# A two-layer graph network on one core: where tile 0's counts stand in the program, and how edge records are rounded

## The chip, the core and the metric

The kernel runs on one core of a Trainium2 chip. A core has five engines that each run their own instruction stream: TensorE (PE in the profile: matrix products and transposes), VectorE (DVE), ScalarE (ACT), GpSimd (POOL) and SyncE (SP, which here only issues transfers). They meet at semaphores. The metric is device microseconds (us) of one execution; lower is better.

## What is computed

There are 6250 nodes with 128 features and 200000 edges, sorted by destination. An attention layer comes first, then two rounds of a relational layer, each over the same edges:

```python
def layer0(h, src, dst, etype):
    e = leaky_relu(score_src[src] + score_dst[dst] + score_rel[etype], 0.01)
    m = segment_max(e, dst)                     # per destination node
    w = exp(e - m[dst])
    alpha = w / segment_sum(w, dst)[dst]
    agg = segment_sum(alpha[:, None] * h[src], dst)
    agg = where(deg > 0, agg, h)
    return agg + h @ loop_weight

x = layernorm(x + layer0(x, src, dst, etype))
h = x
for W_r, W_sl, W_el in two_rounds:
    self_msg = where(in_deg == 0, h @ W_el, h @ W_sl)
    msg = (rel_embed[etype] + h[src]) @ W_r
    h = rrelu(segment_sum(msg, dst) * deg ** -0.5 + self_msg)
return layernorm(x + h)
```

## The kernel before, in words

**Tiles and windows.** The nodes are cut into 50 tiles of 125 (`NT`, `TN`). The edges that end in tile t lie in a window of 4224 edges (`WIN`), held as 128 partitions of 33 columns (`C`). The main loop runs over the tiles; the order of work on every engine is written out by hand, and nothing reorders it.

**What a tile t of the main loop does.** GpSimd gathers the source rows of the window, one indirect transfer for each of the 33 columns (L568), into one of two row buffers; the gathers of tile t wait for the last products of tile t-2 (`acc_c`), since both use the same buffer. SyncE loads the lists of the window: small copies in `load_lists`, and copies of destination and type lists spread to all partitions in `load_wide` (L459). TensorE makes the edge terms with one-hot matrices (`terms`, L781 to L783), ScalarE copies them out, SyncE stores them to memory (L464) and loads them back in another shape (L469, `drw`). On VectorE `terms(t)` (L1146) waits for that load. `weights(t)` (L1156 to L1175) computes the segment maximum, with two short steps on TensorE in between (L870, L875), up to `z`. ScalarE takes the exponent and scales 33 one-hot tiles (L684), TensorE accumulates the attention sum with them (L884, 33 products recorded as 66). VectorE then builds the one-hot lists of the next tile: `prepare_wide(t+1)` (L1109 to L1116, then three L1101) before the sum is read, `prepare_edges(t+1)` (L1131 to L1142) after. `finalize(t)` and `normalise(t)` (L1195 to L1197) give the first layer's output of the tile.

**Counts.** The relational rounds need, for each tile, a matrix that counts edges from every node to the 125 of the tile. It is built in seven batches, `batch(t, 0)` to `batch(t, 6)`: VectorE makes two one-hot tensors for each (L1124 with `idx`), TensorE multiplies them (L814), ScalarE copies the result into the one buffer `AT` (L590, L625, L626), and `store_counts(t)` on SyncE writes `AT` to memory (L475, L477). The first batch of tile t on ScalarE waits for the store of tile t-1 (`at_stored`) and for TensorE's `row(t-1)` (L845 to L847), which also reads `AT`. Products leave TensorE through two pairs of PSUM banks in turn; each use waits for the copy two uses earlier (`before(n)`), in the order of the table `SEQ`.

**Edge records.** The counts are built from records of all edges, made once. `records` on VectorE turns source and destination numbers into two small numbers each (L1251 to L1261, ten instructions on 125 x 1600 elements, from the start of L1251 to `terms(0)`); SyncE stores them (L512); before tile 2's gathers GpSimd fetches them in ten indirect transfers (L560, `recw`); VectorE brings them into shape (L1294, two instructions for each of ten blocks), TensorE transposes them (L899) and ScalarE writes `idx` (L590).

**Where tile 0 stands.** Tile 1's gathers come before the ten transfers of records, tile 2's after. In the loop's first turn, after tile 0's sum and `prepare_edges(1)`, VectorE, TensorE and ScalarE turn the records into `idx` and build tile 0's seven batches, and only then begin `normalise(0)` and tile 1's `terms(1)` and `weights(1)`. SyncE stores tile 0's counts in the same turn, ahead of the lists of tile 3.

**After the loop** TensorE multiplies the stored counts with the node features, twice over (L960), reading them back in pieces; this part runs from about 2160 us to the end.

Of the kernel before, what the change touches and what calls it, by code (L numbers as in the profile page):

```python
# [7 lines left out]
I32 = mybir.dt.int32  # L8
# [5 lines left out]
P = 128  # L14
# [43 lines left out]
SHIFT = 128.0  # L58
NBK = 2
# [45 lines left out]
for t_ in range(NT):  # L105
    if t_ + 1 < NT:
        for k_ in range(QK):
            SEQ["dr", t_ + 1, k_] = len(SEQ)
    if t_ == 0:
        SEQ["types", 1] = len(SEQ)  # L110
        SEQ["turned", 1] = len(SEQ)
        for b_ in range(NGB):
            SEQ["idx", b_] = len(SEQ)
    for j_ in range(BT):
        SEQ["cnt", t_, j_] = len(SEQ)
        if 1 <= t_ < NT - 1 and j_ == 2:
            SEQ["types", t_ + 1] = len(SEQ)
        if 1 <= t_ < NT - 1 and j_ == 3:
            SEQ["turned", t_ + 1] = len(SEQ)
    if t_ in EARLY:  # L120
        SEQ["early", t_] = len(SEQ)
# [29 lines left out]
def build(nc, x, src, dst, etype, emb_rel, loop_w, fc_w, fc2_w, rel_emb, W_r, W_sl, W_el, out):  # L151
    ctx = ExitStack()
    with ctx:
# [96 lines left out]
        lo = carve([P, EW])  # L250
        q_i = lo.bitcast(I32)
        qf = carve([P, EW])
        off = carve([P, EW])
# [123 lines left out]
        def seq(*key):  # L377
            return SEQ[key]
# [5 lines left out]
        def slot(n):  # L384
            return bank[2 + 2 * (n % NBK)]

# [52 lines left out]
        def sp_fast(sp):  # L439
# [73 lines left out]
            for t in range(NT):  # L513
                if t + 2 < NT:
                    f2 = window(t + 2)
                    load_lists(t + 2, f2)
                    load_wide(t + 2, f2)
                if t in EARLY:
                    load_early(t)
                if t + 1 < NT:  # L520
                    reshape_terms(t + 1)
                else:
                    for m in range(RD):
                        load_piece(m)
                if t < NT - 1:
                    store_x1(t)
                store_counts(t)
# [60 lines left out]
        def act_evac(act, n, o, i):  # L588
            act.wait_ge(s("pb"), n + 1)
            act.activation(o, i, ACT.Copy).then_inc(s("ev"), 1)  # L590

        def act_fast(act):
# [79 lines left out]
            for t in range(NT):  # L672
# [19 lines left out]
                if t == 0:  # L692
# [3 lines left out]
                    for b in range(NGB):  # L696
                        n = seq("idx", b)
                        act_evac(act, n, idx[:, b * GB:(b + 1) * GB, :], slot(n)[:, :].rearrange("p (m g) -> p g m", g=GB))
                    for j in range(BT):
                        batch(0, j)  # L700
                    node_t(0)
                    node_a(0, 0)
                elif t < NT - 1:
                    for j in range(3):
                        batch(t, j)
# [48 lines left out]
        def pe_fast(pe):  # L754
# [106 lines left out]
            for t in range(NT):  # L861
# [27 lines left out]
                if 1 <= t < NT - 1:  # L889
                    row(t - 1)  # L890
                if t == 0:
                    types_in(1)
                    types(1)
# [7 lines left out]
                    for j in range(BT):  # L901
                        batch(0, j)
                    x1_in(0)
# [162 lines left out]
        def dve_fast(v, link):  # L1066
# [180 lines left out]
            def records():  # L1247
                v.wait_ge(s("st_l16"), 64)
                v.wait_ge(s("ld_src"), 32)
                a, b, c, i_ = qf[0:EP], lo[0:EP], off[0:EP], srcl[0:EP]  # L1250
                link(v.tensor_scalar(a, i_, 1.0 / TN, -0.496, ALU.mult, ALU.add))  # L1251
                link(v.tensor_copy(q_i[0:EP], a))
                link(v.tensor_copy(a, q_i[0:EP]))
                link(v.scalar_tensor_tensor(b, a, -float(TN), i_, ALU.mult, ALU.add))
                link(v.tensor_scalar(c, b, 0.0, None, ALU.is_lt))
                link(v.tensor_tensor(a, a, c, ALU.subtract))
                link(v.tensor_scalar(c, b, float(TN), None, ALU.is_ge))
                link(v.tensor_tensor(a, a, c, ALU.add))
# [10 lines left out]
            for t in range(NT):  # L1269
# [14 lines left out]
                if t == 0:  # L1284
                    finalize(0)
                    prepare_edges(1)
                    for b in range(NGB):
# [11 lines left out]
                    normalise(0)  # L1299
                elif more:  # L1300
# [11 lines left out]
                else:  # L1312
# [611 lines left out]
```

## Time and profile before

| what | us |
|---|---|
| median of 3 runs | 2772.72 |
| lowest and highest of them | 2772.16, 2774.16 |
| the profiled execution's own time | 2772.09 |
| span of its profile | 2770.1 |
| share of the span: PE, DVE, POOL, ACT | 78%, 74%, 57%, 44% |

The profile follows one execution. Its span begins with the first instruction and ends with the last, so 1.99 us of the execution lie around it. A timeline row gives start, duration, engine, source line, operation and tiles, then how often the row repeats and, in brackets, how long the engine had been idle before it and what released it. A row that stands for several instructions gives the time from the start of the first to the end of the last. DMA_INDIRECT on POOL is the time that GpSimd takes to issue a gather, not the time that the data takes. A row of SPq is the issue of a transfer by SyncE.

### The profile page before, as it was taken

To read this page: it belongs to the slowest core of one execution; us is meant where nothing else is said; L and a number is where in the kernel's file an instruction comes from. 1 tells how busy PE (TensorE), PEld (TensorE's weight loads), DVE (VectorE), ACT (ScalarE), POOL (GpSimd) and SP (SyncE) were. 2 spreads that over 40 slices of the span, in tenths; PEclk is the share of its full clock that TensorE was granted. 3 is DMA by queue.
4 is the path that set the end of the run, shared out by engine and by line. 5 is a ranking of instruction groups with operands and counts; after the bars stand their busy time and mean duration, and the time that the engine had idled before them with its cause. 6 is when DMAs were issued, how large, how long until landed. Compare 5 with 4: busy or idle time off the path is not lost.

```text
span 2770.1 us, 45483 instructions
## 1 busy us (share of the span) xinstructions
PE 2148.2 (78%) x16208; PEld 1803.9 (65%) x16208; DVE 2044.5 (74%) x4582; ACT 1222.7 (44%) x3215; POOL 1590.8 (57%) x1672
## 2 busy tenths in 40 slices
PE   1467666677677677787787788788787999999998
PEld 0355555566566566576676677667666876888887
DVE  6889998888888888898888888888887456333333
ACT  1265566555455555555555555555654323000000
POOL 6767777777777777777777777777774000000000
PEclk9888888888888888888889988999898999999999
DMA  8535554454554554554555555555444344666664
GB/s 222 164 117 166 174 172 141 149 176 146 157 181 145 157 182 150 154 184 152 166 176 157 169 175 164 172 169 174 154 153 153 108 157 135 215 209 212 215 211 158
DMA packets 184632, 463.50 MB, mean 167 GB/s; under 512 B 86336, under 2 KB 113784, under 8 KB 164577
## 3 DMA queue, kind: packets, MB, share of 16 engines
q1 hardware_dynamic: 116050, 339.10, 36.3%
q0 software_dynamic: 53600, 114.17, 15.8%
q10 hardware_dynamic: 14752, 7.26, 1.0%
q8 instruction: 132, 2.16, 0.3%
q14 instruction: 98, 0.80, 0.1%
HBM read 362.54 MB, written 97.84 MB: 166 GB/s over the span
## 4 chain that ended last, share of the span: by engine, by line
POOL 52%; PE 24%; issue 18%; DVE 4%; DMA 2%; ACT 0%; POOLq 0%; ACTq 0%; SPq 0%; DVEq 0%
POOL arena L568 52%; PE pair L960 19%; PE bank L884 1%; DVE arena L1124 1%; PE bank L845 1%; PE pair L933 1%; DMA wlp<-n_L_gnn_loop_weight_dram 1%; PE pair L963 1%; DMA group_starts<-endv 0%; DMA arena<-in_x_dram,srcw 0%; DVE arena L1101 0%; PE pair L814 0%; PE pair L791 0%; DVE arena L1071 0%; DVE arena L1072 0%
## 5 line engine op out<-in xcount | busy, mean ns | idle before, releaser
L568 POOL DMA_INDIRECT arena<-rows,srcw x1617 | 1540.4, 953 | 510.1 <-issue 492.2
L1124 DVE TENSOR_TENSOR arena<-bank,idx 128x2000 bf16<-128x2000 bf16 (+3 forms) x700 | 560.5, 853 | 22.4 <-PE pair L814 19.0
L960 PE MATMUL pair<-arena 125*125 125x384 bf16 x3285 | 551.4, 326 | 1.6 <-DVE arena L1325 1.6
L814 PE MATMUL pair<-arena 128*128 128x250 bf16 x2500 | 344.5, 285 | 262.2 <-DVE arena L1124 208.7
L590 ACT ACTIVATE arena<-pair 99x264 f32<-99x264 f32 (+2 forms) x410 | 278.8, 712 | 582.6 <-PE pair L814 448.9
L960 PEld LDWEIGHTS pair<-arena 125*125 125x125 bf16 x3285 | 447.4, 136 | 103.3 <-issue 8.4
L684 ACT ACTIVATE arena<-arena,wexp 128x128 f32<-128x128 bf16 x1650 | 487.4, 387 | 1.6
L884 PE MATMUL bank<-arena 128*125 128x130 f32 x3300 | 486.9, 319 | 0.0
L884 PEld LDWEIGHTS bank<-arena 128*125 128x125 f32 x3300 | 476.4, 230 | 3.9
L814 PEld LDWEIGHTS pair<-arena 128*128 128x128 bf16 x2500 | 237.8, 102 | 339.7 <-DVE arena L1124 271.5
L1101 DVE TENSOR_TENSOR arena<-arena,bank 128x4224 bf16<-128x4224 int16 x150 | 344.2, 2350 | 1.7
L1323 DVE SCALAR_TENSOR_TENSOR arena<-pair,norm,arena 125x128 f32<-125x128 f32 x99 | 34.6, 350 | 315.3 <-PE pair L963 270.9
L845 PE MATMUL bank<-arena 125*125 125x384 bf16 x1275 | 219.4, 330 | 2.1 <-DVE arena L1213 2.1
L845 PEld LDWEIGHTS bank<-arena 125*125 125x125 bf16 x1275 | 171.0, 137 | 45.2 <-issue 13.9
L791 PE MATMUL pair<-arena 128*125 128x200 bf16 x1650 | 191.8, 288 | 10.1 <-DVE arena L1124 10.1
L791 PEld LDWEIGHTS pair<-arena 128*125 128x125 bf16 x1650 | 190.1, 167 | 12.7 <-issue 10.8
L731 ACT ACTIVATE rstd<-mv,epst 125x1 f32<-125x1 f32 x50 | 14.7, 294 | 406.6 <-DVEq L1365 406.6
L1124 DVE TENSOR_TENSOR arena<-bank,et 128x6600 bf16<-128x6600 bf16 x50 | 179.2, 3584 | 0.0
L625 ACT ACTIVATE arena<-pair 128x500 bf16<-128x500 f32 x150 | 95.7, 638 | 71.9 <-PE pair L814 71.4
L1156 DVE TENSOR_TENSOR u<-arena,dr 128x33 f32<-128x33 f32 x50 | 10.7, 214 | 151.0 <-DMA arena<-rows,srcw 150.8
L1124 DVE TENSOR_TENSOR arena<-bank,dl 128x4224 bf16<-128x4224 bf16 x50 | 117.9, 2358 | 1.7
L804 PE MATMUL bank<-onesb,arena 128*125 128x1 bf16 x50 | 11.4, 229 | 131.1 <-issue 128.6
(250 smaller groups left out, 2311.5 us busy)
## 6 DMA issues: line engine op xcount, KB each, us to landing
arena<-counts SPq DMA_DIRECT2D x106, 812.5 KB, 4.4
counts<-arena SPq DMA_DIRECT2D x50, 1562.5 KB
arena<-dst SPq DMA_DIRECT2D x50, 1056.0 KB
arena<-etype SPq DMA_DIRECT2D x50, 1056.0 KB
arena<-rows,srcw POOLq DMA_INDIRECT x1617
arena<-counts SPq DMA_DIRECT2D x14, 281.2 KB, 2.7
edge_terms<-arena SPq DMA_DIRECT2D x200, 12.4 KB
xt<-in_x_dram SPq DMA_DIRECT2D x50, 62.5 KB
```

The lines of the kernel that those rows point to most:

```text
L568: pool.indirect_dma_start(out=rows[:, q, c, :], out_offset=None, in_=rows0, in_offset=bass.IndirectOffsetOnAxis(ap=srcw[:, q, c:c + 1], ax ...
L590: act.activation(o, i, ACT.Copy).then_inc(s("ev"), 1)
L625: act.activation(AT[:, :, d0:d0 + 2 * G], two, ACT.Copy)
L684: r = act.activation(hot[:, c, :], hotb[:, c, :], ACT.Copy, scale=wexp[:, c:c + 1])
L791: r = pe.matmul(b_[0:TN, 0:R], hotb[:, c, 0:TN], toh[:, c, :], start=(c == 0), stop=(c == C - 1))
L814: r = pe.matmul(group_of(n, gi), ohl[:, sl, gi * GC + c, :], ohm[:, sl, gi * GC + c, :], start=(c == 0), stop=(c == GC - 1))
L845: pe.matmul(o, AT[0:TN, h, :], hs0[0:TN, h, :], start=(h == 0), stop=False)
L884: r = pe.matmul(sums[0:TN, 0:D + 2], hot[:, c, 0:TN], rows[:, q, c, 0:D + 2], start=(c == 0), stop=(c == C - 1))
L960: r = pe.matmul(o, ring[0:TN, m % RD, h - h0, :], hs[k][0:TN, h, :], start=(h == first), stop=(h == last - 1))
L1101: return v.tensor_tensor(out_.rearrange("p (j t) -> p j t", t=2), list_.rearrange("p (j t) -> p j t", t=2), two[:, None, :].broadcast_to(s ...
L1124: return v.tensor_tensor(hot_.rearrange("p c (j t) -> p c j t", t=2), iotap[:, 0:w].rearrange("p (j t) -> p j t", t=2)[:, None, :, :].broa ...
L1323: link(v.scalar_tensor_tensor(o, b_[0:TN, 0:D], n_, acc[0:TN, t, :], ALU.mult, ALU.add))
```

## The change

Two things are changed. First, the step from records to `idx` and the seven batches of tile 0 move from the loop's first turn into its second, on VectorE, TensorE and ScalarE. They now stand behind tile 1's attention weights and sum and behind tile 2's edge terms, and ahead of `row(0)` and of tile 1's own batches. The store of tile 0's counts moves on SyncE behind the lists and edge terms of the second turn; the table `SEQ` follows. Second, `records` rounds the quotient by adding and subtracting 12582912 in one instruction; the six instructions that converted it to integer and back and corrected it by one are gone.

```diff
@@ SEQ
     if t_ == 0:
         SEQ["types", 1] = len(SEQ)
         SEQ["turned", 1] = len(SEQ)
+        continue
+    if t_ == 1:
         for b_ in range(NGB):
             SEQ["idx", b_] = len(SEQ)
+        for j_ in range(BT):
+            SEQ["cnt", 0, j_] = len(SEQ)
@@ SyncE, turn t
                 if t + 1 < NT:
                     reshape_terms(t + 1)
+                    if t == 1:
+                        store_counts(0)
...
-                store_counts(t)
+                if t >= 1:
+                    store_counts(t)
@@ ScalarE, turn t
-                    for b in range(NGB):
-                        n = seq("idx", b)
-                        act_evac(act, n, idx[:, b * GB:(b + 1) * GB, :], slot(n)[:, :].rearrange("p (m g) -> p g m", g=GB))
-                    for j in range(BT):
-                        batch(0, j)
                     node_t(0)
                     node_a(0, 0)
                 elif t < NT - 1:
+                    if t == 1:
+                        for b in range(NGB):
+                            n = seq("idx", b)
+                            act_evac(act, n, idx[:, b * GB:(b + 1) * GB, :], slot(n)[:, :].rearrange("p (m g) -> p g m", g=GB))
+                        for j in range(BT):
+                            batch(0, j)
@@ TensorE, turn t
                 if t + 1 < NT:
                     terms(t + 1)
-                if 1 <= t < NT - 1:
-                    row(t - 1)
-                if t == 0:
-                    types_in(1)
-                    types(1)
+                if t == 1:
                     for b in range(NGB):
                         n = seq("idx", b)
...
                     for j in range(BT):
                         batch(0, j)
+                if 1 <= t < NT - 1:
+                    row(t - 1)
+                if t == 0:
+                    types_in(1)
+                    types(1)
                     x1_in(0)
                     x1_node(0)
@@ VectorE, records
                 link(v.tensor_scalar(a, i_, 1.0 / TN, -0.496, ALU.mult, ALU.add))
-                link(v.tensor_copy(q_i[0:EP], a))
-                link(v.tensor_copy(a, q_i[0:EP]))
-                link(v.scalar_tensor_tensor(b, a, -float(TN), i_, ALU.mult, ALU.add))
-                link(v.tensor_scalar(c, b, 0.0, None, ALU.is_lt))
-                link(v.tensor_tensor(a, a, c, ALU.subtract))
-                link(v.tensor_scalar(c, b, float(TN), None, ALU.is_ge))
-                link(v.tensor_tensor(a, a, c, ALU.add))
+                link(v.tensor_scalar(a, a, TO_WHOLE, TO_WHOLE, ALU.add, ALU.subtract))
@@ VectorE, turn t
                 if t == 0:
                     finalize(0)
                     prepare_edges(1)
+                    normalise(0)
+                if t == 1:
                     for b in range(NGB):
...
                     for j in range(BT):
                         batch(0, j)
-                    normalise(0)
-                elif more:
+                if t >= 1 and more:
                     for j in range(2):
                         batch(t, j)
```

VectorE before, at the end of the loop's first turn: the last one-hot tensors of tile 0's batches, then `normalise(0)` and the edge terms and weights of tile 1 (`u` is their first step).

```order
L1124 TENSOR_TENSOR arena<-bank,idx 128x1500
L1124 TENSOR_TENSOR arena<-bank,idx 128x768
L1195 RECIPROCAL norm<-nv 125x1
L1196 RECIPROCAL nv<-nv 125x1
L1197 TENSOR_SCALAR arena<-arena,mv,nv 125x128
L1146 TENSOR_TENSOR dr<-drw 128x33
L1147 TENSOR_TENSOR dr<-dr,drw 128x33
L1156 TENSOR_TENSOR u<-arena,dr 128x33
```

VectorE in the changed kernel, at the same place: the last steps of `prepare_edges(1)` lead straight into `normalise(0)` and tile 1's terms.

```order
L1147 TENSOR_TENSOR Kx<-dstB 128x32
L1148 TENSOR_SCALAR FS<-dstB 128x33
L1149 TENSOR_SCALAR LS<-dstB 128x33
L1202 RECIPROCAL norm<-nv 125x1
L1203 RECIPROCAL nv<-nv 125x1
L1204 TENSOR_SCALAR arena<-arena,mv,nv 125x128
L1153 TENSOR_TENSOR dr<-drw 128x33
L1154 TENSOR_TENSOR dr<-dr,drw 128x33
L1163 TENSOR_TENSOR u<-arena,dr 128x33
```

The record steps (L1297 now) and the fourteen one-hot tensors of tile 0 that stood between these two places come behind `prepare_wide(2)`.

TensorE before, from the end of tile 1's edge types to tile 1's weights: 40 transposes of records and 50 products of tile 0's counts stand between them.

```order
L798 MATMUL pair<-identb,ctd 128x125
L799 MATMUL pair<-identb,ctd 72x125
L899 MATMUL pair<-ident,arena 128x128 x40
L814 MATMUL pair<-arena 128x250 x50
L833 MATMUL bank<-ident,arena 128x125
L837 MATMUL bank<-wall,nT 125x384
L762 MATMUL bank<-ident,xt 128x125
L870 MATMUL bank<-ident,lf 1x128
```

TensorE in the changed kernel, after tile 2's edge terms (the last of them is the first row) and up to tile 1's own counts and tile 2's edge types.

```order
L789 MATMUL pair<-arena,Zr 3x264
L901 MATMUL pair<-ident,arena 128x128 x40
L820 MATMUL pair<-arena 128x250 x50
L851 MATMUL bank<-arena 125x384
L852 MATMUL bank<-relW,arena 125x384
L853 MATMUL bank<-relW,arena 125x384
L820 MATMUL pair<-arena 128x250 x24
L797 MATMUL pair<-arena 125x200 x33
```

The 90 instructions have moved past tile 1's sum and tile 2's terms, and `row(0)` (L851 to L853) now waits behind them.

SyncE before, from the edge terms of tile 1 into the second turn.

```order
L464 DMA edge_terms<-arena 3x1056 x4
L469 DMA drw<-edge_terms 128x3x33
L481 DMA dense_input<-arena 125x128
L475 DMA counts<-arena 128x6250
L477 DMA counts<-arena 128x250
L444 TENSOR_LOAD plan_i
```

SyncE in the changed kernel, from the edge terms of tile 2 to the end of the second turn.

```order
L466 DMA edge_terms<-arena 3x1056 x4
L471 DMA drw<-edge_terms 128x3x33
L477 DMA counts<-arena 128x6250
L479 DMA counts<-arena 128x250
L483 DMA dense_input<-arena 125x128
L477 DMA counts<-arena 128x6250
L479 DMA counts<-arena 128x250
```

Tile 0's counts have moved one turn on: two stores of counts now stand in the second turn, with only the small store of `dense_input` between them.

## Rows read from the trace of the kernel before

**Rows 1.** The page: shares by engine of the chain that ended last

```profile
POOL 52%; PE 24%; issue 18%; DVE 4%; DMA 2%; ACT 0%; POOLq 0%; ACTq 0%; SPq 0%; DVEq 0%
```

**Rows 2.** Waits of POOL: who waited for whom, total us, times, longest

```profile
POOL arena L568 <- PE bank L884: 9.1, 1, 9.1
```

**Rows 3.** Timeline of POOL: first fetch of records, first gathers of tiles 3 and 4

```profile
115.44 0.98 POOL L560 DMA_INDIRECT arena<-edge_records,gidx  x1 [3.19 <-DMA edge_records<-arena]
...
178.12 0.94 POOL L568 DMA_INDIRECT arena<-rows,srcw  x1 [9.07 <-PE bank L884]
...
219.46 0.94 POOL L568 DMA_INDIRECT arena<-rows,srcw  x1 [0.30 <-issue]
```

**Rows 4.** Timeline of DVE in `records` and at the start of `terms(0)`

```profile
94.44 0.99 DVE L1252 CAST arena<-arena 125x1600 int32<-125x1600 f32 x1
...
98.36 0.99 DVE L1255 TENSOR_SCALAR arena<-arena 125x1600 f32<-125x1600 f32 x1
...
104.14 1.83 DVE L1259 SCALAR_TENSOR_TENSOR arena<-arena 125x1600 f32<-125x1600 f32 x1
...
107.61 0.19 DVE L1146 TENSOR_TENSOR dr<-drw 128x33 f32<-128x33 f32 x1
```

**Rows 5.** Timeline of SyncE's queue: terms of tiles 0, 1, 2 and the records

```profile
99.97 0.39 SPq L469 DMA_DIRECT2D drw<-edge_terms  x1
107.73 0.76 SPq L512 DMA_DIRECT2D edge_records<-arena  x2
...
128.37 2.02 SPq L464 DMA_DIRECT2D edge_terms<-arena  x4
139.73 0.39 SPq L469 DMA_DIRECT2D drw<-edge_terms  x1
...
180.36 1.32 SPq L464 DMA_DIRECT2D edge_terms<-arena  x4
190.07 0.39 SPq L469 DMA_DIRECT2D drw<-edge_terms  x1
```

**Rows 6.** Chain that ended last, two transfers waited for: start, us

```profile
38.00 2.79 DMA gst<-group_starts
...
2075.82 2.58 DMA arena<-rows,srcw
```

**Rows 7.** Timeline of DVE from the end of `prepare_edges(1)` to `terms(2)`

```profile
134.21 0.35 DVE L1294 TENSOR_SCALAR arena<-arena,kcol 128x256 f32<-128x256 f32 x1
...
147.32 0.42 DVE L1237 COPY idx<-arena 128x100 bf16<-128x100 bf16 x2 [1.41 <-ACT arena L590]
...
158.86 0.15 DVE L1195 RECIPROCAL norm<-nv 125x1 f32<-125x1 f32 x1
...
159.37 0.19 DVE L1146 TENSOR_TENSOR dr<-drw 128x33 f32<-128x33 f32 x1
...
162.59 0.35 DVE L1204 SCALAR_TENSOR_TENSOR arena<-bank,iso,slt 125x128 f32<-125x128 f32 x1 [1.94 <-ACT slt L650]
...
166.07 0.29 DVE L1109 TENSOR_TENSOR arena<-xt,bank 125x128 f32<-125x128 f32 x1
...
175.25 0.41 DVE L1237 COPY idx<-arena 128x100 bf16<-128x100 bf16 x2
...
198.15 0.18 DVE L1146 TENSOR_TENSOR dr<-drw 128x33 f32<-128x33 f32 x1
```

**Rows 8.** Timeline of PE: record transposes, sums of tiles 1 and 2

```profile
139.48 2.04 PE L899 MATMUL pair<-ident,arena 128*128 128x128 f32 x12
...
167.75 9.61 PE L884 MATMUL bank<-arena 128*125 128x130 f32 x66
...
179.23 0.38 PE L845 MATMUL bank<-arena 125*125 125x384 bf16 x1
...
187.79 1.85 PE L814 MATMUL pair<-arena 128*128 128x250 bf16 x8 [6.12 <-DVE arena L1124]
...
205.88 9.44 PE L884 MATMUL bank<-arena 128*125 128x130 f32 x66
```

More of the change, by code:

```diff
@@ L58 @@
 SHIFT = 128.0
+TO_WHOLE = 12582912.0
 NBK = 2
@@ L249, in build @@
         here(AT_AT)
-        lo = carve([P, EW])
-        q_i = lo.bitcast(I32)
         qf = carve([P, EW])
-        off = carve([P, EW])
         here(1536)
@@ L1249, in records @@
                 v.wait_ge(s("ld_src"), 32)
-                a, b, c, i_ = qf[0:EP], lo[0:EP], off[0:EP], srcl[0:EP]
+                a, i_ = qf[0:EP], srcl[0:EP]
                 link(v.tensor_scalar(a, i_, 1.0 / TN, -0.496, ALU.mult, ALU.add))
-                link(v.tensor_copy(q_i[0:EP], a))
-                link(v.tensor_copy(a, q_i[0:EP]))
-                link(v.scalar_tensor_tensor(b, a, -float(TN), i_, ALU.mult, ALU.add))
-                link(v.tensor_scalar(c, b, 0.0, None, ALU.is_lt))
-                link(v.tensor_tensor(a, a, c, ALU.subtract))
-                link(v.tensor_scalar(c, b, float(TN), None, ALU.is_ge))
-                link(v.tensor_tensor(a, a, c, ALU.add))
+                link(v.tensor_scalar(a, a, TO_WHOLE, TO_WHOLE, ALU.add, ALU.subtract))
                 v.scalar_tensor_tensor(recs[0:EP, :, GRAN:2 * GRAN], a.rearrange("p (j r) -> p j r", r=GRAN), -float(TN),
@@ L1311, in dve_fast @@
                         batch(t, j)
-                else:
+                if not more:
                     finalize(t)
```

## The prediction

> **What bounds the kernel now.** Read the chain that ended last first. GpSimd holds 52% of it, TensorE 24% [rows 1]: the gathers of the main loop set the pace, and the products after the loop set the rest. So an edit on VectorE or TensorE in the loop counts only where GpSimd waits for it. The waits of GpSimd come next: in the whole loop it waits once for another engine, 9.1 us for TensorE's L884 [rows 2]. The timeline of GpSimd places that wait: the gathers of tile 3 start at 178.12 us, after 9.07 us idle [rows 3]. They need the buffer of tile 1, and tile 1's sum on TensorE ends at 167.75 + 9.61 = 177.36 [rows 8]. From the end of a sum to the first gather it releases is therefore 178.12 - 177.36 = 0.76 us. From there on GpSimd never waits, so its clock at the first gather of tile 4, 219.46 us [rows 3], sets all that follows. The gathers of tile 3 take 219.46 - 178.12 = 41.34 us.
>
> The second thing to read is how near the next such wait is. Tile 4 needs tile 2's sum, which ends at 205.88 + 9.44 = 215.32 [rows 8]. GpSimd could have begun at 216.08, and began at 219.46: **3.38 us** of slack. If the change brings tile 1's sum forward but leaves tile 2's where it is, the wait of 9.07 us only moves to tile 4, and what is gained is those 3.38 us and no more. So the sum below has to find the end of tile 2's sum.
>
> **The records, four instructions in place of ten.** From the start of the second instruction (94.44) to the start of the ninth (104.14) are 9.70 us [rows 4]. One instruction comes back there, a TENSOR_SCALAR on the same shape with 0.99 us [rows 4], about 1.02 with its hand-over. VectorE is 8.7 us shorter and stands at `terms(0)` at 107.61 - 8.7 = 98.9. Should the new one run as slowly as the two-input form (1.83 us [rows 4]) it is 99.8. Neither matters, because `terms(0)` waits for `drw`, whose load is issued only at 99.97 [rows 5], after SyncE's wait for the edge terms; nothing in the change touches that. What it takes to land is not in the trace, as VectorE always came later. The nearest rows are two transfers that were waited for, 2.58 and 2.79 us [rows 6]. I take 2.6 (bounds 2 to 4, four for a queue that is still draining lists). `terms(0)` then starts at 102.6: **5.0 us** early, and not 8.7. All of tile 0's weights and sum shift by 5.0.
>
> SyncE's store of the records was issued at 107.73, when they were ready [rows 5]. It now follows the load of `drw` directly, at about 100.4. In the trace it took 115.44 - 107.73 = 7.7 us until GpSimd went on [rows 3, 5], so it has landed at 108 and the wait of 3.19 us [rows 3] goes. GpSimd then begins the ten fetches at 115.44 - 3.19 = 112.3 or sooner. At its pace of 41.34 / 33 = 1.25 us for one transfer it ends them at 124.8, tile 2's gathers at 166.1 and, if tile 1's sum is done, tile 3's at 207.5. That is 8 us before the release worked out below, so GpSimd's own work has no price.
>
> **Tile 1's weights ahead of tile 0's counts.** The legs, one after the other:
> - `terms(1)` needs its own `drw`. SyncE issued it at 139.73, after 11.36 us from the store of the terms at 128.37 [rows 5]. These follow TensorE, which is 5.0 early: 134.7, and 137.3 with the landing. VectorE, which before began the records at 134.21 [rows 7], is through with `prepare_edges(1)` at 129.2 and, after 0.5 for `normalise(0)` (158.86 to 159.37 [rows 7]), at `terms(1)` at 129.7, so it idles 7.6 us. The transfer is the bound here, which the counts had hidden.
> - From `terms(1)` to the end of `weights(1)`: 166.07 - 159.37 = 6.70 us, of it 1.94 waiting for `slt` [rows 7]. That step of tile 0's node is now made while the transfer is under way, so I take 6.70 - 1.94 + 0.1 = 4.9: 142.2. Upper bound 6.7, if TensorE's small steps are slower after its idle time.
> - To the end of tile 2's edge terms on TensorE: 179.23 - 166.07 = 13.16 [rows 7, 8]: 155.3. Tile 1's sum ends at 177.36 - 23.9 = 153.5, so GpSimd, ready near 166, no longer waits for it.
> - `prepare_wide(2)` ends 9.2 us after the weights, at 151.4, and VectorE can shape only two blocks of records ahead. It waits for TensorE until 155.3. From the first transposes to the copy for tile 0's first batch: 147.32 - 139.48 = 7.84 [rows 7, 8], and I add 0.2 for the copies of the edge terms out of the same PSUM banks: 163.3.
> - Tile 0's batches: 158.86 - 147.32 = 11.54 [rows 7]: 174.9.
> - From tile 1's first batch to `terms(2)`: 198.15 - 175.25 = 22.90 [rows 7]: **197.8**, where the kernel before has 198.15.
>
> So almost all that VectorE is given back it waits away again: 3.7 us at the first `drw`, 7.6 at the second, some 4 for TensorE ahead of the transposes. Tile 2's sum ends 0.35 earlier, at 214.97, and the gathers of tile 4 start at 215.73: 219.46 - 215.73 = **3.7 us** gained. Tile 2's sum ended 215.32 - 177.36 = 38.0 us after tile 1's, the gathers of a tile take 41.3, so there is no third wait, and the gain reaches the end of the loop and the products after it. Against the profiled execution, 2772.09 - 3.7 = 2768.4; its own time lies 0.63 under the median, so against the median 2772.72 - 3.7 = **2769.0**.
>
> **What is costed at nothing.** The store of tile 0's counts has ScalarE's `AT` as its price. It is issued when the last copy is made, near 177, and the store of the same size took 7.7 us [rows 3, 5], so it lands near 184.7. ScalarE's first copy for tile 1 waits for it. TensorE's third batch of tile 1 needs that copy (about 1 us), and before started at 187.79 because VectorE's one-hot tensor was late [rows 8]; now it would be 187.4. The store may land as late as 186.4: 1.7 us of cover. On SyncE nothing but the small store of `dense_input` and tile 1's counts are queued behind it. `row(0)` stands behind the counts and shares this cover.
>
> **The skill and the landing.** The Trainium skill, "DMA: Bandwidth & Descriptors", section "Anatomy of one DMA — SWDGE (gpsimd) path", puts the fixed cost of a transfer issued by GpSimd at about 2.0 us. The trace has 2.58 and 2.79 for small ones [rows 6], a little more. By the page's figure, both landings would be 0.6 shorter, and as an estimate the gain would be 4.9 and not 3.7.
>
> **Rivals.**
> - *The second `drw` comes sooner.* Tile 1's terms took 11.36 us from store to load; tile 2's took 190.07 - 180.36 = 9.71 [rows 5]. Tile 1's list copies overlapped the last of the ten record fetches, which in the changed kernel are issued 3.2 us earlier or more while the lists come 5 us earlier, so much of the overlap stays. At 9.71 the gain is 3.7 + 1.65 = 5.4, with landings of 2.2 us 6.2: about 2766.5. For it: one row at 9.71. The most it could be is where GpSimd itself bounds tile 4, 219.46 - 207.5, some 12 us, and VectorE's own work forbids that.
> - *The hand-overs eat it.* Weights at 6.7 in place of 4.9, a landing of 3 us or more, transposes that wait for more copies: 1.8 + 0.8 + 0.8 = 3.4 us, and the gain is about 0.3. The time is then 2772.4. For it: TensorE is idle before tile 1's weights.
> - *The count store becomes the wait (slower).* `AT` is one buffer and its two uses now lie 0.4 us apart on VectorE. Each us that the store lands after 186.4 delays TensorE's third batch, then the types behind it, and VectorE, by one. The gain is gone at 190.1, 13 us after the issue; a loss of 5.5 us needs 195.6, 18.6 after it. The list copies of a tile took up to 11.4 with all else in flight [rows 5], so I hold it unlikely: 2778 at that point.
> - *The new rounding does nothing for the path.* That is part of my forecast for 3.7 of its 8.7 us; with the old ten instructions the whole chain would be 5.0 later, tile 4 would start at 220.8, and the kernel would be 1.3 slower than before. So the two edits need each other.
>
> **How the numbers follow.** A measurement tells about 0.2%, 5.5 us, from no change. Forecast, a gain of 1 to 5.5: 0.60. Sooner `drw`, a gain over 5.5: 0.20. Hand-overs, from a gain of 1 to a loss of 5.5: 0.16. Slower by over 5.5, the store: 0.04. So faster 0.20, same 0.76, slower 0.04. The range reaches from a gain of 8 (2764.7) to a loss of about 0.5 (2773.2), which leaves out half of the extreme cases on either side.
>
> **What the profile after would show.** VectorE idle some 3.7 us before its first L1153 (`terms(0)`), and some 7 before the second. Tile 1's sum over near 153.5. GpSimd without a wait at tile 3 and with one wait for TensorE at tile 4, of about 8 us (more if the gathers beside the records are issued faster); tile 4's first gather near 215.7. ScalarE's first copy of tile 1's counts behind the store, TensorE's third batch near 187.4. Wrong would be: no wait at tile 4 (gain above 11), a start of tile 4 after 219.5 (a loss), or a further wait of GpSimd in a later tile, which would mean that the loop is not as loose behind tile 4 as I read it.

## The result and the profile after

| what | before | after |
|---|---|---|
| median, us | 2773.84 | 2769.09 |
| lowest and highest, us | 2769.97, 2775.00 | 2766.67, 2770.64 |
| runs | 22 | 22 |
| the profiled execution | 2772.09 | 2769.03 |
| span of its profile | 2770.1 | 2767.0 |

The ratio after to before is 0.9985, with a 95% interval of 0.9979 to 0.9991. The changed kernel is some 4.7 us faster (2.5 to 5.8), which is less than the 0.2% that was named as the bound for "no change". The two profiled executions differ by 3.1 us. One execution of all those reported here, of `records_terms_first_b` below, ran slow (3030.98 us, at a granted TensorE clock of 0.726 of full speed where the others have 0.905 to 0.908), and its median is taken without it.

The chain that ended last kept its shares to within a point; this row answers to [rows 1]:

```profile
POOL 52%; PE 25%; issue 18%; DVE 3%; DMA 1%; ACT 0%; SPq 0%; POOLq 0%; DVEq 0%; ACTq 0%
```

The waits of GpSimd (who waited for whom, total us, times, longest) answer to [rows 2], and its timeline to [rows 3]:

```profile
POOL arena L573 <- PE bank L890: 12.8, 1, 12.8
...
POOL arena L565 <- DMA edge_records<-arena: 1.1, 1, 1.1
```

```profile
108.14 0.94 POOL L565 DMA_INDIRECT arena<-edge_records,gidx  x1 [1.07 <-DMA edge_records<-arena]
...
120.64 0.94 POOL L573 DMA_INDIRECT arena<-rows,srcw  x1 [0.30 <-issue]
...
215.61 0.95 POOL L573 DMA_INDIRECT arena<-rows,srcw  x1 [12.76 <-PE bank L890]
```

There is still exactly one wait for TensorE, but it stands at tile 4 (215.61) and no longer at tile 3. It is longer than before, 12.76 us and not 9.07, and GpSimd is nevertheless earlier: 219.46 - 215.61 = 3.85 us at tile 4's first gather. A longer wait is no loss when it replaces a later start.

The timeline of VectorE, from `records` to tile 2's terms, answers to [rows 4] and [rows 7]. L1153 is the first step of `terms`, L1116 the first step behind the weights, L1297 the shaping of the records, L1244 the first step of a batch:

```profile
94.17 0.99 DVE L1259 TENSOR_SCALAR arena<-arena 125x1600 f32<-125x1600 f32 x1
...
96.94 1.82 DVE L1262 SCALAR_TENSOR_TENSOR arena<-arena 125x1600 f32<-125x1600 int32 x1
101.80 0.19 DVE L1153 TENSOR_TENSOR dr<-drw 128x33 f32<-128x33 f32 x1 [3.03 <-DMA drw<-edge_terms]
...
135.48 0.19 DVE L1153 TENSOR_TENSOR dr<-drw 128x33 f32<-128x33 f32 x1 [6.94 <-DMA drw<-edge_terms]
...
140.85 0.28 DVE L1116 TENSOR_TENSOR arena<-xt,bank 125x128 f32<-125x128 f32 x1
...
155.73 0.35 DVE L1297 TENSOR_SCALAR arena<-arena,kcol 128x256 f32<-128x256 f32 x1 [4.50 <-PE pair L901]
...
162.60 0.42 DVE L1244 COPY idx<-arena 128x100 bf16<-128x100 bf16 x2 [1.38 <-ACT arena L595]
...
174.14 0.41 DVE L1244 COPY idx<-arena 128x100 bf16<-128x100 bf16 x2
...
197.58 0.18 DVE L1153 TENSOR_TENSOR dr<-drw 128x33 f32<-128x33 f32 x1
```

SyncE's queue and TensorE, which answer to [rows 5] and [rows 8]; L466 stores edge terms, L471 loads `drw`, L890 is the attention sum of a tile, L901 the transposes of the records:

```profile
99.74 0.39 SPq L471 DMA_DIRECT2D drw<-edge_terms  x1
100.17 0.93 SPq L514 DMA_DIRECT2D edge_records<-arena  x2
...
122.10 1.79 SPq L466 DMA_DIRECT2D edge_terms<-arena  x4
133.43 0.39 SPq L471 DMA_DIRECT2D drw<-edge_terms  x1
...
176.13 0.35 SPq L477 DMA_DIRECT2D counts<-arena  x1
```

```profile
142.53 10.26 PE L890 MATMUL bank<-arena 128*125 128x130 f32 x66
154.99 1.06 PE L901 MATMUL pair<-ident,arena 128*128 128x128 f32 x8 [0.26 <-ACT arena L595]
...
186.68 1.85 PE L820 MATMUL pair<-arena 128*128 128x250 bf16 x8 [7.50 <-DVE arena L1131]
...
205.19 9.67 PE L890 MATMUL bank<-arena 128*125 128x130 f32 x66
```

Tile 1's sum ends at 142.53 + 10.26 = 152.79, which is 24.6 us earlier than before (177.36). Tile 2's sum ends at 205.19 + 9.67 = 214.86, 0.46 earlier (215.32), and it is tile 2's sum that now releases GpSimd. The landing of `drw` can be read for the first time, since VectorE now waits for it: 101.80 - 99.74 = 2.06 us, and 135.48 - 133.43 = 2.05.

### The profile page after: what moved, and what is told of

The parts are those of the page before. It is cut to its first block, busy times and chain, and to the rows that moved or that the text cites. A ratio compares the mean times of both kernels' runs of the same rounds, so it can differ in the third digit from the quotient of the medians.

```text
span 2767.0 us, 45477 instructions
## 1 busy us (share of the span) xinstructions
PE 2150.3 (78%) x16208; PEld 1809.1 (65%) x16208; DVE 2036.9 (74%) x4576; ACT 1221.9 (44%) x3215; POOL 1585.9 (57%) x1672
## 4 chain that ended last, share of the span: by engine, by line
POOL 52%; PE 25%; issue 18%; DVE 3%; DMA 1%; ACT 0%; SPq 0%; POOLq 0%; DVEq 0%; ACTq 0%
POOL arena L573 51%; PE pair L967 19%; PE bank L890 2%; POOL arena L553 1%; DVE arena L1131 1%; PE pair L940 1%; PE bank L851 1%; DMA edge_terms<-arena 1%; PE pair L970 1%; PE pair L820 0%; DMA arena<-in_x_dram,srcw 0%; DVE arena L1108 0%; ACT arena L595 0%; PE pair L797 0%; DVE arena L1078 0%
## 5 line engine op out<-in xcount | busy, mean ns | idle before, releaser
L890 PE MATMUL bank<-arena 128*125 128x130 f32 x3300 | 491.0, 322 | 0.0
L890 PEld LDWEIGHTS bank<-arena 128*125 128x125 f32 x3300 | 482.5, 234 | 2.1
L851 PE MATMUL bank<-arena 125*125 125x384 bf16 x1275 | 219.2, 329 | 3.1 <-DVE arena L1220 2.0
L851 PEld LDWEIGHTS bank<-arena 125*125 125x125 bf16 x1275 | 170.9, 137 | 46.3 <-issue 13.7
L797 PEld LDWEIGHTS pair<-arena 128*125 128x125 bf16 x1650 | 190.1, 167 | 12.5 <-issue 10.8
L1163 DVE TENSOR_TENSOR u<-arena,dr 128x33 f32<-128x33 f32 x50 | 10.7, 214 | 141.8 <-DMA arena<-rows,srcw 141.5
```

The source lines that it names most:

```text
L797: r = pe.matmul(b_[0:TN, 0:R], hotb[:, c, 0:TN], toh[:, c, :], start=(c == 0), stop=(c == C - 1))
L851: pe.matmul(o, AT[0:TN, h, :], hs0[0:TN, h, :], start=(h == 0), stop=False)
L890: r = pe.matmul(sums[0:TN, 0:D + 2], hot[:, c, 0:TN], rows[:, q, c, 0:D + 2], start=(c == 0), stop=(c == C - 1))
```

## Experiments

Two questions were open. Which of the two edits pays, and do they need each other, as the prediction's fourth rival says? And is the chain through `drw` really what is left? Each quoted expectation says what its theories are. One theory is the prediction's own reading throughout: `terms(0)` is bound by the transfer, not by VectorE's instructions, and what GpSimd gains is what arrives at tile 4.

### The records alone, and the order alone

`records_only_b` is the kernel before with the short rounding. Line numbers are its own: L885 is the sum, L569 the gathers.

```diff
-                link(v.tensor_copy(q_i[0:EP], a))
...
-                link(v.tensor_tensor(a, a, c, ALU.add))
+                link(v.tensor_scalar(a, a, TO_WHOLE, TO_WHOLE, ALU.add, ALU.subtract))
```

`order_only_b` is the changed kernel with the ten instructions put back, the same diff read backwards.

> The order of before with the four-instruction records alone, once more. Theory A (the slack theory with the legs as the changed kernel's trace gives them): terms(0) starts at 101.8, 5.8 us earlier than before, tile 1's sum ends at 171.5, tile 3's gathers start at 172.3 and tile 4's at 172.3 + 41.3 = 213.6, bounded by GpSimd, because tile 2's sum ends at 209.5: a gain of 5.8 us, more than the 4 of the whole change, so the new order costs about 2. Theory B (my prediction's words, the two edits need each other): a gain of 0 to 1 us.

> The new order with the ten-instruction records, once more. Theory A: from terms(0) to tile 4's gathers the changed kernel needs 215.61 - 101.80 = 113.8 us; with terms(0) at 107.6 tile 4 starts at 221.4, so 2 us slower than before, one wait of GpSimd of about 11 us at tile 4, none at tile 3. Rival (the order itself is what gained): 3 to 4 us faster than before.

**Measured, records alone:** 2767.60 us (10 runs) beside 2772.33 for the kernel before (19 runs), ratio 0.9984 (0.9974 to 0.9993). **Order alone:** 2772.66 us (10 runs), ratio 1.0002 (0.9992 to 1.0012). Timelines of `records_only_b`, VectorE at `terms(0)`, TensorE's sums of tiles 1 and 2, and GpSimd at tiles 3 and 4:

```profile
101.79 0.20 DVE L1147 TENSOR_TENSOR dr<-drw 128x33 f32<-128x33 f32 x1 [3.20 <-DMA drw<-edge_terms]
```

```profile
161.83 10.24 PE L885 MATMUL bank<-arena 128*125 128x130 f32 x66
...
200.57 9.66 PE L885 MATMUL bank<-arena 128*125 128x130 f32 x66
```

```profile
172.83 0.94 POOL L569 DMA_INDIRECT arena<-rows,srcw  x1 [10.95 <-PE bank L885]
...
214.04 0.95 POOL L569 DMA_INDIRECT arena<-rows,srcw  x1 [0.30 <-issue]
```

`terms(0)` starts at the same 101.8 us as in the changed kernel, 5.8 earlier than before, and tile 1's sum ends 5.3 earlier (172.07 and not 177.36). GpSimd still waits at tile 3, until 172.83, and starts tile 4 at 214.04: 5.4 us earlier than before, and 1.6 earlier than in the changed kernel. Tile 2's sum ends at 210.23, well ahead. Theory A had tile 4 at 213.6 and a gain of 5.8; theory B, a gain of 0 to 1, is out.

The waits of GpSimd in `order_only_b`, and its timeline at tile 4:

```profile
POOL arena L576 <- PE bank L893: 8.3, 2, 8.0
```

```profile
218.64 0.94 POOL L576 DMA_INDIRECT arena<-rows,srcw  x1 [8.04 <-PE bank L893]
```

Neither theory had this number: theory A said 221.4, the rival some 216. From `terms(0)` (107.95) to tile 4 this execution needs 110.7 us, where the changed kernel needed 113.8. Of the 3.1 us, 1.2 are gained up to `terms(1)`, mostly on SyncE's queue (10.48 us from store to load and not 11.33), 0.8 between there and tile 0's first batch, and 0.9 in tile 1's batches. The 0.8 are TensorE's sum of tile 1:

```profile
147.49 9.44 PE L893 MATMUL bank<-arena 128*125 128x130 f32 x66
```

It took 9.44 us at a mean granted clock of 0.85 over that stretch, and 10.26 at 0.73 in the changed kernel. The other kernels follow in the same order: 9.50 us at 0.79, 9.61 at 0.78 (the kernel before), 9.68 and 9.71 at 0.77, 10.24 at 0.73, 10.38 at 0.72. So up to 0.9 us of a leg goes with the clock that an execution happened to have there, and a difference of 1 or 2 us at tile 4 between two single executions isn't yet a difference between two kernels.

**What follows.** The order alone brings tile 4 forward by 0.8 us (219.46 to 218.64) in one execution, which no median shows. The records alone bring as much as both together: 4.7 us in the medians each. So the two edits don't need each other. The records do it alone, and the new order adds nothing that these runs can tell.

### Three instructions more in the records

If the transfer bounds `terms(0)`, instructions put back into `records` must be free as long as VectorE stays ahead of it. VectorE idles 3.03 us there, three instructions of 0.99 us fill that.

```diff
+        spare_w = carve([P, EW])
...
                 link(v.tensor_scalar(a, a, TO_WHOLE, TO_WHOLE, ALU.add, ALU.subtract))
+                for _ in range(3):
+                    link(v.tensor_scalar(spare_w[0:EP], a, 1.0, None, ALU.mult))
```

> The changed kernel with three more instructions of 1.0 us on 125 x 1600 elements in records, into a tile that nobody reads. Theory A (terms(0) waits 3.03 us for drw, so work of that size is free there): terms(0) at 101.8 to 101.9, tile 4's gathers at 215.6 to 215.8. Rival (what VectorE does there counts fully): terms(0) 3.1 later, tile 4's gathers at 218.7.

**Measured:** one run of 2764.49 us. SyncE's queue, VectorE and GpSimd in `three_more`:

```profile
98.05 0.39 SPq L472 DMA_DIRECT2D drw<-edge_terms  x1
```

```profile
100.06 0.20 DVE L1154 TENSOR_TENSOR dr<-drw 128x33 f32<-128x33 f32 x1
```

```profile
212.78 0.94 POOL L574 DMA_INDIRECT arena<-rows,srcw  x1 [10.35 <-PE bank L891]
```

This execution had issued the load 1.69 us earlier than the changed kernel's (98.05 and 99.74), ahead of anything that the edit touches, so it is read from that load on. `terms(0)` follows it by 2.01 us (2.06 in the changed kernel), now without an idle stretch. VectorE's own last large step ahead of the records, its 128x6600 tensor, is as far off as before: 100.06 - 87.33 = 12.73 us, against 101.80 - 89.09 = 12.71, where the rival wanted 3.1 more. From `terms(0)` to tile 4 are 212.78 - 100.06 = 112.72 us, against 215.61 - 101.80 = 113.81, which is within what this stretch scatters (110.7 us in `order_only_b`). So at `terms(0)` the three instructions cost nothing: of the 8.7 us that the rounding takes off VectorE, 3 are worth nothing here, and what pays are the other 5.7, down to the landing. The total is one run. It lies below all 22 of the changed kernel (2766.67 at the lowest), with the earlier start, and measures no cost of this size.

### The store of tile 0's counts, made slow

The prediction's slower rival was that ScalarE's one buffer `AT` is still being stored when tile 1 wants it. The store goes out three times, and ScalarE waits for the last copy:

```diff
+        again = dram("counts_again", (2, P, HI * TN), BF16)
...
+                if t == 0:
+                    for k in range(2):
+                        sp.dma_start(again[k], AT[:, :, :].rearrange("p h d -> p (h d)")).then_inc(s("again"), 16)
...
+                    if t == 1:
+                        act.wait_ge(s("again"), 32)
```

> The changed kernel, where tile 0's counts are stored three times (twice more to memory that nobody reads) and ScalarE's first copy for tile 1 waits for all three. Theory A (cover of the store): the three land near 191, ScalarE's first copy starts there (182.2 in the changed kernel), TensorE's third batch of tile 1 at about 192 (186.7), tile 4's gathers near 220.6 (215.6): each us past 185.6 costs one. Rival (other waits cover more): tile 4's gathers under 217.

**Measured:** one run of 2773.71 us. ScalarE's first copies of tile 1's counts in the changed kernel, and then in `store_thrice` with TensorE's third batch and GpSimd at tile 4:

```profile
182.21 1.96 ACT L595 ACTIVATE arena<-pair 128x1000 bf16<-128x1000 f32 x2 [6.11 <-DMA counts<-arena]
```

```profile
190.27 1.96 ACT L599 ACTIVATE arena<-pair 128x1000 bf16<-128x1000 f32 x2 [15.47 <-DMA counts<-arena]
```

```profile
191.45 1.82 PE L826 MATMUL pair<-arena 128*128 128x250 bf16 x8 [13.57 <-ACT arena L599]
```

```profile
220.52 0.94 POOL L577 DMA_INDIRECT arena<-rows,srcw  x1 [16.81 <-PE bank L896]
```

The mechanism is as the prediction told it. With the last store landed at 190.27 TensorE's third batch waits for ScalarE and no longer for VectorE, it starts 191.45 - 186.68 = 4.8 us later, and tile 4 is 220.52 - 215.61 = 4.9 us later, which is past the kernel before. In the changed kernel the store had landed by 182.21, 6.1 us after its issue at 176.13, and the third batch started at 186.68 for VectorE's sake. It needs 1.18 us of copying behind the landing (190.27 to 191.45 above), which leaves 186.68 - 182.21 - 1.18 = 3.3 us of cover.

### The edge terms ahead of the list copies

Of the three long waits of VectorE on the changed path two are for `drw` (3.03 and 6.94 us; the third, 4.50, is for TensorE's transposes), and the long leg of `drw` is on SyncE's queue: from the store of the terms to the load there are 9.3 us for tile 0 (90.48 to 99.74) and 11.3 for tile 1 (122.10 to 133.43). Ahead of the store in the queue stand two list copies of 1056 KB each. Two kernels put them behind the terms, in the changed order (`order_terms_first_b`) and with the order of before and the short rounding (`records_terms_first_b`):

```diff
-            load_wide(1, f1)
             reshape_terms(0)
+            load_wide(1, f1)
...
-                    load_wide(t + 2, f2)
+                    if t > 0:
+                        load_wide(t + 2, f2)
                 if t + 1 < NT:
                     reshape_terms(t + 1)
+                    if t == 0:
+                        load_wide(2, f2)
```

> The changed kernel, with the edge terms of tiles 0 and 1 stored and loaded back ahead of the wide list copies of tiles 1 and 2 on SyncE's queue. Theory A (the lists ahead in the queue hold the terms 9 to 11 us): terms(0) at about 98.8 without a wait, terms(1) at about 125 in place of 135.5. weights(1) then waits for TensorE's product of node 0, which stands behind tile 1's edge types, until about 132, so z of tile 1 is some 4.4 us earlier than in the changed kernel, tile 4's gathers start near 211, a gain of 8 us against before. Rival (the wait is the terms' own way through memory): terms(0) stays at 101.8, gain as in the changed kernel, 4 us.

> The order of before, four-instruction records, terms ahead of the lists on SyncE's queue. Theory A: terms(0) at 98.8, 3.0 us earlier than with the records alone, so tile 3's gathers at 172.8 - 3.0 = 169.8 and tile 4's at 211.1, bounded by GpSimd: a gain of 7.5 to 8.5 us. Rival (the list copies of tile 1, now issued some 4 us later, hold prepare_wide(1)): a gain as with the records alone, 4 to 5 us.

**Measured:** in the changed order 2763.34 us (6 runs), ratio 0.9971 (0.9960 to 0.9983); in the order of before 2761.73 us (5 runs), ratio 0.9964 (0.9951 to 0.9976). The kernel before took 2771.63 beside them (12 runs). SyncE's queue and GpSimd at tiles 3 and 4 in `records_terms_first_b`:

```profile
89.63 1.20 SPq L465 DMA_DIRECT2D edge_terms<-arena  x4
92.33 0.39 SPq L470 DMA_DIRECT2D drw<-edge_terms  x1
92.89 0.37 SPq L460 DMA_DIRECT2D arena<-dst  x1
```

```profile
167.53 0.94 POOL L572 DMA_INDIRECT arena<-rows,srcw  x1 [6.48 <-PE bank L888]
...
208.87 0.94 POOL L572 DMA_INDIRECT arena<-rows,srcw  x1 [0.30 <-issue]
```

And in `order_terms_first_b`, SyncE's queue for tile 1, VectorE at the two `terms` and GpSimd at tile 4:

```profile
117.41 1.23 SPq L466 DMA_DIRECT2D edge_terms<-arena  x4
121.95 0.39 SPq L471 DMA_DIRECT2D drw<-edge_terms  x1
```

```profile
97.65 0.19 DVE L1156 TENSOR_TENSOR dr<-drw 128x33 f32<-128x33 f32 x1
...
124.33 0.19 DVE L1156 TENSOR_TENSOR dr<-drw 128x33 f32<-128x33 f32 x1
```

```profile
208.73 0.94 POOL L576 DMA_INDIRECT arena<-rows,srcw  x1 [7.63 <-PE bank L893]
```

Tile 0's leg is 2.7 us (89.63 to 92.33) in place of 9.3, tile 1's 4.5 (117.41 to 121.95) in place of 11.3. VectorE has no wait for `drw` left at either place, in either kernel; its own work is the bound there again. Tile 4 starts 10.7 us earlier than before in the changed order and 10.6 in the old one, and the medians are 8.3 and 9.9 us under the kernel before, where the change itself gained 4.7. Both beat the kernel before. Against the changed kernel they are some 3.6 and 5.2 us ahead, each taken in relation to the kernel before; the second is clear of the noise, the first only just, since its interval (up to 0.9983) touches that of the changed kernel (from 0.9979). Between the two nothing is told apart, since their intervals overlap. Theory A was right in both on the wait, and had tile 4 some 2.2 us later than it came (211 and 211.1). Part of what tile 4 shows is that these two executions were ahead before the edit: VectorE's 128x6600 tensor ahead of the records starts at 88.10 and 88.87 us, against 89.09 in the changed kernel.

### The same edits where another part is the bound

Four of the kernels first ran on a chip on which the kernel before itself takes 4487.59 us (35 runs).

> The order of before with the four-instruction records alone. Theory A (the slack theory with the legs as the changed kernel's trace gives them): terms(0) starts at 101.8, 5.8 us earlier than before, tile 1's sum ends at 171.5, tile 3's gathers start at 172.3 and tile 4's at 172.3 + 41.3 = 213.6, bounded by GpSimd, because tile 2's sum ends at 209.5: a gain of 5.8 us, more than the 4 of the whole change, so the new order costs about 2. Theory B (my prediction's words, the two edits need each other; the records' 8.7 us do nothing without the new order): a gain of 0 to 1 us.

> The new order with the ten-instruction records. Theory A: from terms(0) to tile 4's gathers the changed kernel needs 215.61 - 101.80 = 113.8 us; with terms(0) at 107.6 tile 4 starts at 221.4, so 2 us slower than before, one wait of GpSimd of about 11 us at tile 4, none at tile 3. Rival (the order itself is what gained): 3 to 4 us faster than before.

> The changed kernel, with the edge terms of tiles 0 and 1 stored and loaded back ahead of the wide list copies of tiles 1 and 2 on SyncE's queue. Theory A (the lists ahead in the queue hold the terms 9 to 11 us): terms(0) at about 98.8 without a wait, terms(1) at about 125 in place of 135.5. Then weights(1) waits for TensorE's product of node 0, which stands behind tile 1's edge types, until about 132, so z of tile 1 is some 4.4 us earlier than in the changed kernel, tile 4's gathers start near 211, a gain of 8 us against before. Rival (the wait is the terms' own way through memory): terms(0) stays at 101.8, gain as in the changed kernel, 4 us.

> The order of before, four-instruction records, terms ahead of the lists on SyncE's queue. Theory A: terms(0) at 98.8, the whole chain 8.8 us earlier than before, tile 3's gathers at about 169.4, tile 4's at 210.7 bounded by GpSimd: a gain of 8.8 us. Rival (the list copies of tile 1, now started some 4 us later, hold prepare_wide(1)): a gain of 5 to 6 us.

**Measured**, as ratio to the kernel before there: records alone 1.0001 (0.9985 to 1.0017), order alone 1.0033 (1.0016 to 1.0051), order with the terms first 1.0026 (1.0009 to 1.0042), records with the terms first 1.0015 (1.0000 to 1.0030). The gains that were expected do not come: none of the theories quoted above holds there. The waits of GpSimd in `records_only` and its chain by engine say why they could not:

```profile
POOL arena L569 <- PE bank L885: 1659.9, 48, 46.7
```

```profile
another core or an unknown queue 39%; PE 33%; DVE 15%; issue 9%; ACT 4%; DMA 1%; ACTq 0%; SPq 0%; DVEq 0%
```

GpSimd waits for TensorE in 48 tiles and not in one. GpSimd is not in the chain at all, so where it stands at tile 4 decides nothing. The granted clock is 0.743 there and 0.905 in `records_only_b`, the same program on the first chip, but TensorE is only 2329.1 - 2148.7 = 180 us longer busy, of 1720 us by which the span is longer. 39% of the chain are waits to which the profile can give no releaser. What holds these engines back on that chip stays open. The runs test nothing of the theory above. They show that a gain taken from one bound is gone where the bound is another, and that the moved counts even cost some 0.3% there.

## Why the prediction was right, and where it was not

**The median.** 2769.0 was forecast from 2772.72; 2769.09 came out beside 2773.84, a gain of 4.7 us, and it lies in the forecast's band of 1 to 5.5. That the two medians agree within 0.1 us is luck: the gain was forecast 1.0 us too small, and the kernel before, in 22 runs and not 3, came out 1.1 us slower than the 2772.72 that the forecast started from.

**The slack (right).** The wait of tile 3 went to tile 4, and 3.85 us of gain arrived there where 3.7 were forecast. That only the slack of 3.38 us and the little by which tile 2's sum moves are paid out, out of 24.6 us by which tile 1's sum moved, was the step that carried the forecast, and it holds.

**The legs (right in sum, each a little off).**

| place | forecast | measured |
|---|---|---|
| `terms(0)` | 102.6 | 101.80 |
| `terms(1)` | 137.3 | 135.48 |
| end of `weights(1)` | 142.2 | 140.85 |
| end of tile 1's sum | 153.5 | 152.79 |
| first batch of tile 0 | 163.3 | 162.60 |
| first batch of tile 1 | 174.9 | 174.14 |
| `terms(2)` | 197.8 | 197.58 |
| end of tile 2's sum | 214.97 | 214.86 |
| tile 4's first gather | 215.73 | 215.61 |

The lead of 1.8 us at `terms(1)` was given back on the way. The weights took 5.4 us in place of 4.9: the copy of `cc` waits for TensorE 0.4 us longer than before. 0.65 went between the weights and the first batch of tile 0, where tile 1's sum took 10.26 us and not 9.61, and 0.54 in tile 1's batches (23.44 and not 22.90).

**The landing of `drw` (mis-sized).** I took 2.6 us; it is 2.05 and 2.06. The figure of about 2.0 us in the Trainium skill, "DMA: Bandwidth & Descriptors", section "Anatomy of one DMA — SWDGE (gpsimd) path", was the nearer one, though it is told there of transfers that GpSimd issues and this one is issued by SyncE. The gain of 4.9 us worked out from it did not come at tile 4, where 3.85 were measured, because the rest of the legs took it back.

**The sooner `drw` (did not happen in the profiled execution).** Tile 1's leg stayed at 11.33 us, where it was 11.36. The rival wanted 9.71. It is less settled than it looks, as this leg scatters: in `store_thrice`, whose program is the same up to there, it took 9.77.

```profile
123.23 1.73 SPq L467 DMA_DIRECT2D edge_terms<-arena  x4
133.00 0.39 SPq L472 DMA_DIRECT2D drw<-edge_terms  x1
```

The other kernels with the lists ahead had 9.85, 10.47 and 10.48. So it may be partly luck that the sum came out so near at tile 4: the profiled execution drew a long leg. The gain that the rival forecast, 5.4 us, lies in the interval of the measured one (2.5 to 5.8), and the medians can't exclude it.

**GpSimd's wait (mis-sized, no price).** 8 us were forecast, 12.76 came. The gathers beside `records` are issued faster, as there are fewer slow instructions beside them, and GpSimd reaches the record fetches at 108.14, not at 112.3. It would have been there 1.07 us sooner still: the wait for the records, which the prediction had gone, is shorter and not gone. The ten fetches end 10 x 1.25 = 12.5 later, at 120.64, and all of that time is spent waiting at tile 4.

**"So the two edits need each other" (wrong).** The fourth rival priced the new order with the ten old instructions, at tile 4 = 220.8, and concluded from one of the two cases. It never priced the other: the old order with the short rounding. By the prediction's own numbers all of the old chain would be 5.0 earlier, with the release at tile 3 at 178.12 - 5.0 = 173.1 and tile 4 at 173.1 + 41.34 = 214.5, better than its forecast of 215.73 for both. Measured are 172.83 and 214.04. The other case was off too: 218.64 and not 220.8, of which tile 1's queue leg (10.48 us and not 11.36) and its landing (1.96 and not 2.6) make 1.5.

**The store of the counts (right that it is covered).** Forecast: landed at 184.7, tolerated until 186.4. Measured: 182.21, with 3.3 us of cover and not 1.7. What happens beyond it, `store_thrice` shows.

**Behind tile 4.** At tile 4 the two profiled executions lie 3.85 us apart, at the last gather of the loop 2.8 and at the end 3.1, while the medians are 4.7 apart. GpSimd never waits in between. From tile 4's first gather to the last there are 1897.6 us before and 1898.7 after, for the same 1518 gathers; a single issue took 946.1 ns in the mean before and 946.8 after, and that accounts for 1.06 of the 1.08 us. In the eight kernels traced at about 2770 us the stretch takes 1897.1 to 1899.4 us. So a difference of 1 or 2 us at the end of two profiled executions is the scatter of the gathers' issue. The other gap has a plainer reason: the profiled execution of the kernel before (2772.09) was 1.75 us faster than its median, that of the changed kernel (2769.03) was at its own.

## What to carry over

When a wait is to be removed, first find how far the next one is: the gain is paid out only up to that slack, however far the first dependence moves. Price each edit of a pair alone in both directions before saying that they need each other. And when the engine on the path turns out to be waiting for a small transfer, look at what stands ahead of it in its queue: putting two large copies behind it was worth another 3.5 to 5 us here, about as much as the whole change. A gain of a few us read from two single executions needs a second look: here one leg alone differed by 1.6 us between two executions of the same instructions.

## What the hardware did that I had not expected

**The issue of a gather depends on what VectorE runs.** Most issues take 0.94 us. The timeline of GpSimd in the kernel before, and that of VectorE beside it:

```profile
23.32 0.95 POOL L548 DMA_INDIRECT arena<-in_x_dram,srcw  x1 [0.30 <-issue]
24.57 4.14 POOL L548 DMA_INDIRECT arena<-in_x_dram,srcw  x1 [0.30 <-issue]
29.01 0.95 POOL L548 DMA_INDIRECT arena<-in_x_dram,srcw  x1 [0.30 <-issue]
```

```profile
24.41 3.48 DVE L1035 TENSOR_TENSOR arena<-arena 125x3200 f32<-125x3200 f32 x1
27.92 3.49 DVE L1036 TENSOR_REDUCE arena<-arena 125x25 f32<-125x3200 f32 x1
```

The gather issued at 24.57 ends at 28.71, after the TENSOR_TENSOR at 27.89, and the next, beside the TENSOR_REDUCE, takes 0.95. Outside `records` the kernel before has four such pairs, a gather issued while an f32 TENSOR_TENSOR of 1.2 to 3.5 us was running (at 24.57, 32.76, 60.87 and 67.03 us), and each of these gathers ends 0.82 or 0.83 us after the TENSOR_TENSOR. In `records_only` on the other chip VectorE came to the first of these instructions only at 51.69 us, when the last gather of that stretch had been issued (45.92), and no gather from 18 us to there took more than 0.95. Beside `records` the issues took 1.41 to 2.59 us before and 1.36 to 1.55 after. That is how a change on VectorE made GpSimd faster without touching it. No run tested which property of the instruction does it.

**A small load behind two large copies.** From the issue of the store of edge terms to the issue of the load there were 2.7 and 2.8 us for tile 0 and 4.0 and 4.5 for tile 1 with no list copies directly ahead of them, and 8.9 to 9.4 for tile 0 and 9.8 to 11.4 for tile 1 behind two copies of 1056 KB on the same queue. Once issued, the load landed in 1.9 to 2.1 us.

**Two chips, one program.** 2772 and 4488 us for the kernel before. Of the short rounding alone there is a trace on both. The issue of most gathers takes 0.94 us on both and VectorE is busy 2037.8 and 2041.0 us in all; TensorE's products for the counts take 320 ns in the mean at the granted clock of 0.743, and 284 at 0.905. The waits are what differs most: GpSimd waits 1660 us for TensorE there, and 11 here.
